# Modulations by column groups, an ordered first load and a buffer for the first projection weights, in a four-layer conditioned transformer

## The chip, the cores and the metric

The kernel runs on one core of one Trainium2 chip. The metric is the device time of one execution in microseconds (us), the median over runs. Engines are named as in the profile: PE is TensorE (PEld its weight loads), DVE VectorE, ACT ScalarE, POOL GpSimd, SP SyncE, which here issues every DMA.

## The reference

Sixteen sequences of 256 tokens with 256 features go through four transformer blocks, each conditioned on a vector per sequence. What concerns us is how the condition enters; layer 0, cut to that:

```
cond = silu(c) @ wc.T + bc                     # c: 16 x 256, wc: 1536 x 256
sh1, sc1, g1, sh2, sc2, g2 = split(cond, 6)
h = _ln(x) * (1 + sc1) + sh1;  x = x + g1 * attention(h)
h = _ln(x) * (1 + sc2) + sh2;  x = x + g2 * mlp(h)
```

Layers 1 and 2 are of the same kind, with a gain and an offset of the norm (`g1`, `be1`, ...) folded in, attention causal in layer 1 and with biases in layer 2. Layer 3 (called ROPE in the code) has no gates g; its condition goes through two products, `t1 = time_emb @ w_t1 + b_t1` (256 to 512 columns), then `(t1[:, :256] * silu(t1[:, 256:])) @ w_t2 + b_t2` (256 to 1024 columns), which give two scales and two shifts.

## The kernel before, in words

The program has two parts, each a block in which every engine has its own instruction list, with a barrier of all engines between them.

**The first part, here called the prologue,** makes everything that depends on the condition, for all four layers: COND, the scale and shift of each layer with features on the partitions (8 columns of 16 sequences per layer), and GR, the gate rows with sequences on the partitions, which go to DRAM (`gate_scratch`). SC is silu of the condition (L326 on ACT), stationary or moving with 16 columns. For each layer PE makes the gates (L353: the condition stationary, 256 weight columns moving, 4 products) and the scales and shifts (L360: 128 x 128 blocks of the weights stationary, the 16 columns of the condition moving, 16 products). L346 is the first product of ROPE. DVE turns the results into GR (L387, L391) and COND (L401 to L405, four short instructions for each of 4 feature halves, one waiting for another). In the lists the layers come as 0, 1, 2, ROPE. The loads are issued by SP on one queue in the order in which they are written: the weights CW of layer 0 (1536 KB), half of the input X (2048 KB), CW of layers 1 and 2, `cw_t1` and `cw_t2` of ROPE (they lie in the upper half of X until they are used), then the first projection weights through the two small buffers RAW, each buffer reused once its contents are split. An fp32 weight is split in two halves, "h" by ACT (`split_hi`, L252) and "l" by POOL or DVE (`split_lo`, L258), since the main part multiplies in fp32r. The upper half of X is loaded when the last layer's product is done (L306).

**The second part** is a software pipeline over 64 tiles (4 layers of 16 sequences). In step t the tile t+1 is normalised and projected to queries, keys and values (L948, L592, L924, L994, L483), tile t attends (L530 scores, L969 maxima, L729 transposed scores, L895 exponentials, L752 values), tile t-1 goes through the output projection and its norm, tile t-2 through the MLP. The first step is t = -2; in step -1 only tile 0 is projected. A table `plan` says in which step, and at which of three places in it (FIRST, EARLY, LATE), which chunk of the next weights is split; `load_raw` issues the loads for it. SP copies queries and keys into stacked operands QS and KS (L1356, 24 DMAs a tile) and the row maxima into QS (L1323). The order of work on each engine is fixed as written; nothing is scheduled at run time.

## Time and profile before

| | us |
|---|---|
| median of 3 runs (lowest, highest) | 2271.77 (2271.73, 2272.78) |
| the profiled execution, its own time | 2277.37 |
| its span in the profile | 2275.6 |
| PE busy in the span | 2175.1 (96%) |
| the prologue, from the span's start to the first instruction of the second part (DVE, 56.53) | 56.5 |
| the first main projection of PE (L483) starts at | 68.58 |

The page divides the span into busy time by engine and shows PE busy for 96% of it. It is an average: two stretches at the start are far from it, and the views by time show them. A wait is written in brackets behind the row, with the instruction or DMA that ended it.

### The profile page before, as it was taken

The numbers are of one execution on the slowest core, as the hardware profiler recorded it, in microseconds if no ns is written. First come the engines' busy times: TensorE is split into PE (matmuls) and PEld (weight loads), VectorE is DVE, ScalarE is ACT, GpSimd is POOL, SyncE is SP. The second block draws the span as 40 slices with busy tenths as digits, with TensorE's granted clock in tenths as the row PEclk, the third lists the DMA queues.
The fourth block names the chain that finished last, engine by engine and source line by source line (L and its number), as shares of the span: only waits on it lengthen the run. The fifth ranks groups of instructions, "written<-read, shape, count | busy, mean of one in ns | idle before, by whom it ended". The sixth has DMA issues, their size and how long they took to land.

```text
span 2275.6 us, 63435 instructions
## 1 busy us (share of the span) xinstructions
PE 2175.1 (96%) x20136; PEld 1830.7 (80%) x20136; DVE 1701.5 (75%) x4378; ACT 1251.0 (55%) x2620; POOL 1087.2 (48%) x1333
## 2 busy tenths in 40 slices
PE   7599999999999999999999999999999999999997
PEld 6478888888878888888878888888777878787877
DVE  3477777777777777777787777777888888888873
ACT  0356666666665556555676666666655443535341
POOL 1235544455445544454555544455454444444444
PEclk9899999999999999999999999999999999999999
DMA  6322222122322222112331222112222111211210
GB/s 200 110 69 65 67 70 72 64 63 81 95 81 64 68 70 67 62 62 92 90 99 64 70 74 67 63 61 80 82 79 65 59 64 60 61 64 58 68 57 15
DMA packets 164960, 166.12 MB, mean 73 GB/s; under 512 B 29328, under 2 KB 144400, under 8 KB 164848
## 3 DMA queue, kind: packets, MB, share of 16 engines
q1 hardware_dynamic: 164848, 164.69, 22.8%
q8 instruction: 63, 1.03, 0.2%
q14 instruction: 49, 0.40, 0.1%
HBM read 58.47 MB, written 4.39 MB: 28 GB/s over the span
## 4 chain that ended last, share of the span: by engine, by line
PE 84%; DVE 6%; issue 3%; SPq 2%; ACT 1%; DMA 1%; POOL 1%; POOLq 0%; ACTq 0%; DVEq 0%
PE B L483 36%; PE B L583 14%; PE B L752 10%; PE B L729 7%; PE B L530 7%; PE B L592 4%; PE B L602 2%; SPq L1356 2%; PE B L686 2%; DVE NEGM L969 2%; PE B L507 2%; DVE G L976 1%; ACT PR L895 1%; DMA RAW<-in_w 1%; ACT G L865 0%
## 5 line engine op out<-in xcount | busy, mean ns | idle before, releaser
L895 ACT ACTIVATE PR<-B 128x512 f32<-128x512 f32 (+1 forms) x1024 | 505.0, 570 | 285.0 <-PE B L729 282.2
L1251 POOL TENSOR_TENSOR GHl<-G,GHh 128x256 fp32r<-128x256 f32 x512 | 377.6, 738 | 476.2 <-ACT GHh L871 290.1
L969 DVE TENSOR_REDUCE NEGM<-B 128x2 f32<-128x512 f32 x768 | 485.1, 683 | 94.2 <-PE B L530 94.2
L483 PE MATMUL B<-H2h,W1h 128*128 128x256 f32 x1280 | 397.6, 311 | 3.1 <-issue 3.1
L483 PE MATMUL B<-H2h,W1l 128*128 128x256 f32 x1280 | 363.1, 284 | 0.0
L483 PE MATMUL B<-H2l,W1h 128*128 128x256 f32 x1280 | 362.5, 283 | 0.0
L871 ACT ACTIVATE G<-B,VEC 128x256 f32<-128x256 f32 x384 | 182.0, 474 | 284.4 <-PE B L483 284.4
L583 PE MATMUL B<-W2h,GHh 128*128 128x256 f32 x1024 | 296.8, 290 | 1.7 <-POOL GHl L1251 1.7
L583 PE MATMUL B<-W2l,GHh 128*128 128x256 f32 x1024 | 290.0, 283 | 0.0
L583 PE MATMUL B<-W2h,GHl 128*128 128x256 f32 x1024 | 289.4, 283 | 0.0
L483 PEld LDWEIGHTS B<-H2h,W1h 128*128 128x128 f32 x1280 | 244.4, 191 | 44.3 <-issue 26.2
L752 PE MATMUL B<-PR,V 128*32 128x256 f32 (+1 forms) x4096 | 262.2, 374 | 14.1 <-ACT PR L895 8.7
L483 PEld LDWEIGHTS B<-H2l,W1h 128*128 128x128 f32 x1280 | 245.3, 192 | 0.0
L483 PEld LDWEIGHTS B<-H2h,W1l 128*128 128x128 f32 x1280 | 244.4, 191 | 0.0
L1281 POOL TENSOR_TENSOR H2l<-HF,H2h 128x512 fp32r<-128x512 f32 x64 | 82.1, 1283 | 333.9 <-DVE H2h L1105 333.9
L729 PE MATMUL B<-QS,KS 64*128 64x256 f32 (+1 forms) x2048 | 211.6, 309 | 10.8 <-ACT PR L895 2.0
L530 PE MATMUL B<-KS,QS 48*128 48x256 f32 (+1 forms) x2048 | 199.0, 311 | 20.8 <-DMA KS<-KHL 13.2
L729 PEld LDWEIGHTS B<-QS,KS 64*128 64x128 f32 x2048 | 145.9, 186 | 82.5 <-ACT PR L895 48.3
L583 PEld LDWEIGHTS B<-W2h,GHh 128*128 128x128 f32 x1024 | 195.4, 191 | 10.3 <-DVE GHh L981 2.1
L966 DVE CUSTOM_DVE_ANT_0 B<-B,MASK 128x128 f32<-128x128 f32 (+1 forms) x512 | 165.8, 392 | 41.1 <-PE B L530 41.1
L583 PEld LDWEIGHTS B<-W2l,GHh 128*128 128x128 f32 x1024 | 196.0, 191 | 0.0
L583 PEld LDWEIGHTS B<-W2h,GHl 128*128 128x128 f32 x1024 | 195.9, 191 | 0.0
(149 smaller groups left out, 4753.1 us busy)
## 6 DMA issues: line engine op xcount, KB each, us to landing
QS<-QHL SPq DMA_DIRECT2D x768, 64.0 KB, 2.1
KS<-KHL SPq DMA_DIRECT2D x768, 64.0 KB, 2.1
GA<-gate_scratch SPq DMA_DIRECT2D x48, 256.0 KB, 3.2
GM<-gate_scratch SPq DMA_DIRECT2D x48, 256.0 KB, 3.5
RAW<-in_w SPq DMA_DIRECT2D x36, 256.0 KB, 3.1
CW<-in_cw SPq DMA_DIRECT2D x3, 1536.0 KB, 13.3
X<-in_x SPq DMA_DIRECT2D x2, 2048.0 KB, 10.4
QS<-MT SPq DMA_DIRECT2D x256, 4.0 KB
```

Of the source, the lines that this page charges most:

```text
L483: last = nc.tensor.matmul(dst, w[i], x[j], start=(first_k and n == 0), stop=(last_k and n == 2))
L530: last = nc.tensor.matmul(bank(banks[h])[:, i, 0:keys], QS[b:b + STK, p, i * P:(i + 1) * P], KS[b:b + STK, p, 0:keys], start=True, stop=True)
L583: last = nc.tensor.matmul(bank(7)[:, i, :], GH[x][:, j % RING, i * P:(i + 1) * P], W2[y][:, j, :], start=(j == 0 and n == 0 and i == 0), s ...
L592: last = nc.tensor.transpose(dst[:, f, i * P:(i + 1) * P], src[:, i, f * P:(f + 1) * P], IDENT[:])
L729: last = nc.tensor.matmul(B[:, banks[h], k * T:k * T + T - first], KS[b:b + ROWS, p, k * P:(k + 1) * P], QS[b:b + ROWS, p, first:T], start ...
L752: last = nc.tensor.matmul(bank(6 + g // 2)[32 * j:32 * j + 32, g % 2, c], V[:, k, HV * h:HV * h + 32], PR[:, h % PRING, k, 0:n], start=(k ...
L871: last = nc.scalar.activation(dst[:, j % RING, :], bank(3 - j % 2)[:, 0, :], ACT.Gelu, bias=VEC[:, s.lm, V_B1 + j:V_B1 + j + 1])
L895: nc.scalar.activation(PR[:, h % PRING].rearrange("p k q -> p (k q)")[:, 0:n], src[:, 0:n], ACT.Exp, scale=SCALE).then_inc(ac_exp, 1)
L966: last = nc.vector.tensor_tensor_reduce(src[:, i, 0:keys], src[:, i, 0:keys], unmasked, -1.0, HIGHEST, ALU.add, ALU.min, NEGM[:, i, c:c + 1])
L969: last = nc.vector.tensor_reduce(NEGM[:, :, c], src, op=ALU.max, axis=AX.X, negate=True)
L1251: nc.gpsimd.tensor_tensor(GH[1][:, j % RING, :], G[:, j % RING, :], GH[0][:, j % RING, :].bitcast(F32), ALU.subtract).then_inc(po_gl, 1)
L1281: nc.gpsimd.tensor_tensor(H2[1][:], HF[:], H2[0][:].bitcast(F32), ALU.subtract).then_inc(po_h2, 1)
```

## The change

It has three parts, and a shift of the plan that goes with them.

1. **Modulations.** The scales and shifts are made with the condition stationary, as the gates are: SC and Z3 are padded with zeros to 32 columns, and the four groups of 256 weight columns go to the four 32-column groups of PE's array (L366, 8 products of 32 x 256 per layer instead of 16 of 128 x 16). The result has sequences on the partitions; DVE copies it (MOD, L438), PE transposes it in two 128 x 128 pieces (L382), and DVE makes COND with 5 instructions of 64 elements (L445 to L451) instead of 16 of 16. The layers come as 0, 1, ROPE, 2, and in each the gates come behind the modulation on PE, and behind COND on DVE.
2. **Loads in another order.** One sequence of X only, then the first weights, then the layers as they are used, with `cw_t1` ahead of layer 1 and `cw_t2` ahead of layer 2; the rest of the lower half of X comes last. The upper half (2048 KB) and the gate rows' way to DRAM move into the second part.
3. **First projection weights** in buffers EQ and EO of their own, loaded whole and split with 3 instructions on ACT and POOL instead of 5 each through RAW.
4. In `plan` the four groups of MLP weights of layer 0 move by one step: from steps -1 and 0 to steps 0 and 1.

Core of the diff:

```diff

-        plan = {(-1, EARLY): part(0, "1", 0, 2), (-1, LATE): part(0, "2", 0, 1),
-                (0, EARLY): part(0, "1", 1, 3), (0, LATE): part(0, "2", 2, 3)}
+        plan = {(0, EARLY): part(0, "1", 0, 2), (0, LATE): part(0, "2", 0, 1),
...
+            EQ, EO = esb("EQ", [P, KD, WQ_COLS[0]]), esb("EO", [P, KD, D])
+            SC = esb("SC", [P, KD, 32])
...
+            Z3 = esb("Z3", [P, KD, 32])
+            MOD = [esb(f"MOD{i}", [P, D]) for i in range(2)]
...
+            t1tile = bank(7, 32)
+            LAYERS = (0, 1, ROPE, 2)
...
+                def modulation(l):
                     sp.dma_start(CW[l][:], a[f"cw{l}"].rearrange("(k p) n -> p k n", p=P)).then_inc(sp_cw[l], 16)
                     sp.dma_start(RB[l], a["rows"][l].partition_broadcast(NSEQ)).then_inc(sp_cw[l], 16)
...
+                sp.dma_start(CT[:], a["c_t"]).then_inc(sp_ct, 16)
+                sp.dma_start(VEC[:], a["vec"]).then_inc(sp_cw[0], 16)
+                sp.dma_start(IDENT[:], a["ident"]).then_inc(sp_cw[0], 16)
+                modulation(0)
+                sp.dma_start(X[:, 0:1], x_in[:, 0:1]).then_inc(sp_x[0], 16)
+                sp.dma_start(EQ[:], a["wq0"].rearrange("(k p) n -> p k n", p=P)).then_inc(sp_first[0], 16)
+                sp.dma_start(EO[:], a["wo0"].rearrange("(k p) n -> p k n", p=P)).then_inc(sp_first[1], 16)
                 sp.dma_start(CT1, a["cw_t1"].rearrange("(k p) n -> p k n", p=P)).then_inc(sp_cw[ROPE], 16)
+                modulation(1)
                 sp.dma_start(CT2, a["cw_t2"].rearrange("(k p) n -> p k n", p=P)).then_inc(sp_cw[ROPE], 16)
-                load_raw(sp, range(len(first_weights)))
-                sp.dma_start(IDENT[:], a["ident"]).then_inc(sp_const, 16)
+                modulation(2)
+                sp.dma_start(X[:, 1:8], x_in[:, 1:8]).then_inc(sp_x[1], 16)
                 sp.dma_start(ROT[:], a["rot"]).then_inc(sp_const, 16)
                 sp.dma_start(MASK[:], a["mask"]).then_inc(sp_const, 16)
...
-                sp.dma_start(X[:, 8:16], x_in[:, 8:16]).then_inc(sp_x[1], 16)
-                sp.wait_ge(sp_gs, 16)
-                sp.wait_ge(sp_x[0], 16)
-                sp.wait_ge(sp_const, 64)
-
...
+                nc.gpsimd.memset(SC[:], 0.0).then_inc(po_init, 1)
+                nc.gpsimd.memset(Z3[:], 0.0).then_inc(po_init, 1)
...
+                for k in range(KD):
+                    po.wait_ge(ac_first, k + 1)
+                    nc.gpsimd.tensor_tensor(WQ[0][1][:, k, :], EQ[:, k, :], WQ[0][0][:, k, :].bitcast(F32),
+                                            ALU.subtract).then_inc(po_first, 1)
...
+                nc.scalar.activation(SC[:, :, 0:NSEQ], CT[:], ACT.Silu).then_inc(ac_silu, 1)
+                ac.wait_ge(sp_first[0], 16)
+                for k in range(KD):
+                    nc.scalar.activation(WQ[0][0][:, k, :], EQ[:, k, :], ACT.Copy).then_inc(ac_first, 1)
+                ac.wait_ge(sp_first[1], 16)
+                nc.scalar.activation(WO[0][:], EO[:], ACT.Copy).then_inc(ac_first, 1)
...
+                def conditioning():
+
+                    pe.wait_ge(sp_cw[ROPE], 32)
+                    for f in range(2 * KD):
+                        for k in range(KD):
+                            last = nc.tensor.matmul(t1tile[:, f, :], CT1[:, k, f * P:(f + 1) * P], CT[:, k, :],
+                                                    start=(k == 0), stop=(k == KD - 1))
+                    last.then_inc(pe_t1, 1)
+
+                def modulation(l):
+
+                    w, m = (CT2, Z3) if l == ROPE else (CW[l], SC)
+                    for k in range(KD):
+                        for c, c0 in enumerate(starts[l]):
+                            last = nc.tensor.matmul(B[32 * c:32 * c + 32, l, 0:D], m[:, k, :], w[:, k, c0:c0 + D],
+                                                    start=(k == 0), stop=(k == KD - 1))
+                    last.then_inc(pe_mod, 1)
+
...
+                    for r, c0 in enumerate((2 * D, 5 * D)):
+                        for k in range(KD):
+                            last = nc.tensor.matmul(bank(4 + l)[0:NSEQ, r, :], SC[:, k, 0:NSEQ], CW[l][:, k, c0:c0 + D],
+                                                    start=(k == 0), stop=(k == KD - 1))
+                    last.then_inc(pe_gates, 1)
...
+                    pe.wait_ge(dv_mod, n + 1)
+                    for f in range(KD):
+                        last = nc.tensor.transpose(bank(l, 4)[:, 2 + f, :], MOD[n % 2][:, f * P:(f + 1) * P], IDENT[:])
+                    last.then_inc(pe_cond, 1)
+
+                pe.wait_ge(ac_silu, 1)
+                pe.wait_ge(po_init, 2)
+                for n, l in enumerate(LAYERS):
                     if l == ROPE:
-                        for f in range(2 * KD):
-                            for k in range(KD):
...
-                        pe.wait_ge(vz, KD)
+                        pe.wait_ge(dv_t1, KD)
                     else:
...
-                    w, m = (CT2, Z3) if l == ROPE else (CW[l], SC)
-                    for c, c0 in enumerate(starts[l]):
-                        for f in range(KD):
-                            for k in range(KD):
-                                last = nc.tensor.matmul(ctile[l][:, 2 * c + f, :],
-                                                        w[:, k, c0 + f * P:c0 + (f + 1) * P], m[:, k, :],
-                                                        start=(k == 0), stop=(k == KD - 1))
-                    last.then_inc(pm, 1)
+                        pe.wait_ge(sp_cw[l], 64 if l == 0 else 32)
...
+                    modulation(l)
+                    if l != ROPE:
+                        gates(l)
+                    to_features(n, l)
+                    if n == 0:
+                        conditioning()
...
+                        dv.wait_ge(ac_t1, KD)
...
-                            nc.vector.scalar_tensor_tensor(Z3[:, k, :], t1tile[:, k, :], VEC[:, ROPE, V_T1 + k:V_T1 + k + 1],
-                                                           SLU[:, k, :], ALU.add, ALU.mult).then_inc(vz, 1)
-                    else:
...
-
-                    dv.wait_ge(pm, 1 + l)
...
-                            chain(nc.vector.tensor_scalar(U[:, f, :], ctile[l][:, tile, :], vec(sc), 1.0, ALU.add, ALU.add))
-                            chain(nc.vector.tensor_scalar(U2[:, f, :], ctile[l][:, tile + KD, :], vec(sh), None, ALU.add))
-                            settle()
-                            chain(nc.vector.tensor_scalar(COND[:, l, cs + f, :], U[:, f, :], vec(g), None, ALU.mult))
-                            chain(nc.vector.scalar_tensor_tensor(COND[:, l, cb + f, :], U[:, f, :], vec(be), U2[:, f, :],
-                                                                 ALU.mult, ALU.add))
-                            settle()
...
+                            nc.vector.scalar_tensor_tensor(Z3[:, k, 0:NSEQ], t1tile[:, k, :], VEC[:, ROPE, V_T1 + k:V_T1 + k + 1],
...
+                    dv.wait_ge(pe_mod, i + 1)
+                    nc.vector.tensor_copy(MOD[i % 2][:], B[:, l, 0:D]).then_inc(dv_mod, 1)
+                    dv.wait_ge(pe_cond, i + 1)
...
+                    chain(nc.vector.tensor_tensor(U[:], sc, SCP[:, l].unsqueeze(3).to_broadcast([P, 2, KD, NSEQ]), ALU.add))
+                    chain(nc.vector.tensor_tensor(U2[:], sh, shift, ALU.add))
+                    settle()
+                    chain(nc.vector.tensor_tensor(cond[:, :, 0], U[:], gain, ALU.mult))
+                    chain(nc.vector.tensor_tensor(U3[:], U[:], offset, ALU.mult))
+                    settle()
+                    chain(nc.vector.tensor_tensor(cond[:, :, 1], U3[:], U2[:], ALU.add))
+                    settle()
+                    if l != ROPE:
+                        gate_rows(l, l + 1)
...
+                    if isinstance(a_, int) and a_ == 0:
+                        ac.wait_ge(sp_gs, 16)
...
+                    if isinstance(tile, int) and tile in (0, 1, 3):
+                        dv.wait_ge(sp_x[(0, 1, None, 2)[tile]], 16)
...
+                    if isinstance(s.q, int) and s.q == 0:
+                        sp.dma_start(X[:, 8:16], a["x"].rearrange("s (t p) d -> p s t d", p=P)[:, 8:16]).then_inc(sp_x[2], 16)
+                        sp.wait_ge(sp_const, 48)
...
+            sp.wait_ge(dv_rows, 6)
+            sp.dma_start(g_scr.rearrange("l s r d -> s l r d"), GR).then_inc(sp_gs, 16)
```

The first place is PE in the prologue. Of before, all layers but the last product (CW and `X<-in_cw_t` are the weights, SC the condition, `sp_cw3` the semaphore that both ROPE weights raise):

```order
L353 MATMUL B<-CW,SC 16x256 x3
L360 MATMUL B<-SC,CW 128x16 x16
L353 MATMUL B<-CW,SC 16x256 [waits sp_cw1]
L353 MATMUL B<-CW,SC 16x256 x3
L360 MATMUL B<-SC,CW 128x16 x16
L353 MATMUL B<-CW,SC 16x256 [waits sp_cw2]
L353 MATMUL B<-CW,SC 16x256 x3
L360 MATMUL B<-SC,CW 128x16 x16
L346 MATMUL B<-CT,X 128x16 [waits sp_cw3]
L346 MATMUL B<-CT,X 128x16 x7
L360 MATMUL B<-Z,X 128x16 [waits dv_t1]
```

Now, from the transposes of layer 0 to those of ROPE:

```order
L382 MATMUL B<-IDENT,MOD 128x128 [waits dv_mod]
L382 MATMUL B<-IDENT,MOD 128x128
L357 MATMUL B<-CT,X 128x16 [waits sp_cw3]
L357 MATMUL B<-CT,X 128x16 x7
L366 MATMUL B<-CW,SC 32x256 [waits sp_cw1]
L366 MATMUL B<-CW,SC 32x256 x7
L374 MATMUL B<-CW,SC 16x256 x4
L382 MATMUL B<-IDENT,MOD 128x128 [waits dv_mod]
L382 MATMUL B<-IDENT,MOD 128x128
L366 MATMUL B<-X,Z 32x256 [waits dv_t1]
L366 MATMUL B<-X,Z 32x256 x7
L382 MATMUL B<-IDENT,MOD 128x128 [waits dv_mod]
```

The block product (L360) is gone, and two waits stand in PE's list that did not: the ROPE product L357 waits for both ROPE weights ahead of layer 1, and each pair of transposes waits for DVE's copy.

The second place is DVE from the barrier to the first tile's query. Before (XQ is the normalised tile, W1l the low half of an MLP weight):

```order
L935 BN_STATS ST<-X 128x6 x2
L940 BN_AGGR MV<-ST 128x2 [waits dv_st1]
L940 BN_AGGR MV<-ST 128x2
L258 TENSOR_TENSOR W1l<-RAW,W1h 128x512 [waits ac_w] x2
L948 TENSOR_SCALAR XQ<-X,MV,RS 128x256 [waits po_rs1]
L948 TENSOR_SCALAR XQ<-X,MV,RS 128x256
L994 CAST H1h<-HF 128x512 [waits ac_h1]
L1198 CAST QHL<-B 128x512 [waits pe_q]
```

Now:

```order
L984 BN_STATS ST<-X 128x6 [waits sp_x0]
L984 BN_STATS ST<-X 128x6
L989 BN_AGGR MV<-ST 128x2 [waits dv_st1]
L989 BN_AGGR MV<-ST 128x2
L997 TENSOR_SCALAR XQ<-X,MV,RS 128x256 [waits po_rs1]
L997 TENSOR_SCALAR XQ<-X,MV,RS 128x256
L1043 CAST H1h<-HF 128x512 [waits ac_h1]
L1247 CAST QHL<-B 128x512 [waits pe_q]
```

The two splits W1l ahead of XQ are gone from here; the next pair comes in step 0 as before, and there is one more pair in step 1.

The third place is SP from the first tile's last key copies to the row maxima (MT) of tile 0. Before, and behind it now:

```order
L1356 DMA KS<-KHL 16x4x256 [waits dv_k]
L1356 DMA KS<-KHL 16x4x256 x5
L239 DMA RAW<-in_w 128x2x256 [waits dv_w] x2
L1323 DMA QS<-MT 1x4x256 [waits ac_mt]
L1323 DMA QS<-MT 1x4x256
L1331 DMA GA<-gate_scratch 128x512
L1323 DMA QS<-MT 1x4x256 [waits ac_mt]
```

```order
L1407 DMA KS<-KHL 16x4x256 [waits dv_k]
L1407 DMA KS<-KHL 16x4x256 x5
L1411 DMA X<-in_x 128x16x256
L240 DMA RAW<-in_w 128x2x256 [waits dv_w,sp_const]
L240 DMA RAW<-in_w 128x2x256 [waits dv_w]
L1372 DMA QS<-MT 1x4x256 [waits ac_mt]
L1372 DMA QS<-MT 1x4x256
L1382 DMA GA<-gate_scratch 128x512 [waits sp_gs]
```

The 2048 KB of X stand between the key copies and the loads of W2 (`RAW<-in_w 128x2x256`), and ahead of the rows of maxima.

## Rows read from the trace of the kernel before

**Rows 1.** Windows of the prologue's middle: busy us (instructions) of each engine, PEclk, DMA

```profile
20.00:30.00 10.00, 10.00 (x39) 7.47 (x40) 4.49 (x20) 1.03 (x2) 1.00 (x2) 1.00 0.81 298
```

**Rows 2.** Timeline of the prologue: start, us, engine, what [idle before <-releaser]

```profile
9.83 3.57 PE L353 MATMUL B<-CW,SC 128*16 128x256 f32 x8 [9.83 <-ACT SC L326]
13.33 7.01 PE L360 MATMUL B<-SC,CW 128*128 128x16 f32 x32
13.44 0.74 DVE L387 TENSOR_TENSOR PR<-B,PR 16x256 f32<-16x256 f32 x2 [13.44 <-PE B L353]
14.22 0.74 DVE L391 TENSOR_TENSOR PR<-PR 16x256 f32<-16x256 f32 x2
...
41.12 3.57 PE L346 MATMUL B<-CT,X 128*128 128x16 f32 x16
...
45.27 0.38 DVE L381 SCALAR_TENSOR_TENSOR Z<-B,VEC,SLU 128x16 f32<-128x16 f32 x2 [0.71 <-ACT SLU L332]
...
55.76 0.23 DVE L405 SCALAR_TENSOR_TENSOR COND<-U,VEC 128x16 f32<-128x16 f32 x1
```

**Rows 3.** Timeline, SP's issues of three loads in the prologue

```profile
2.13 0.46 SPq L292 DMA_DIRECT2D PR<-in_rows  x1
...
3.11 6.05 SPq L291 DMA_DIRECT2D CW<-in_cw  x1
...
11.53 0.47 SPq L296 DMA_DIRECT2D X<-in_cw_t  x1
```

**Rows 4.** DMA issues: KB, us from issue to landing, of the first and third of these

```profile
PR<-in_rows SPq DMA_DIRECT2D x1, 64.0 KB, 7.3
```

```profile
X<-in_cw_t SPq DMA_DIRECT2D x1, 1024.0 KB, 16.4
```

**Rows 5.** Timeline at 414 us, the column groups of L752 and the weight load behind

```profile
414.39 1.07 PE L752 MATMUL B<-PR,V 128*32 128x256 f32 x16
```

```profile
415.39 0.54 PEld L729 LDWEIGHTS B<-QS,KS 64*128 64x128 f32 x8 [0.41 <-ACT PR L895]
```

**Rows 6.** Windows of PE's projections: PE's busy us (x), then the others, PEclk, DMA

```profile
71.00:72.00 1.00, 1.00 (x7) 1.00 (x6) 0.48 (x1) 0.00 (x0) 0.00 (x0) 1.00 0.71 223
95.00:96.00 1.00, 1.00 (x7) 1.00 (x7) 1.00 (x2) 0.73 (x2) 0.71 (x1) 0.50 0.01 4
98.00:99.00 1.00, 1.00 (x10) 1.00 (x9) 0.70 (x2) 1.00 (x3) 0.00 (x0) 1.00 0.00 0
```

**Rows 7.** Timeline of the first tile

```profile
58.12 0.71 POOL L1222 TENSOR_TENSOR RS<-TV,HALF 128x2 f32<-128x2 f32 x1
...
62.40 1.35 DVE L258 TENSOR_TENSOR W1l<-RAW,W1h 128x512 fp32r<-128x512 f32 x2 [4.77 <-ACT W1h L252]
63.66 0.73 DVE L948 TENSOR_SCALAR XQ<-X,MV,RS 128x256 f32<-128x256 f32 x2
64.45 1.12 PE L592 MATMUL B<-IDENT,XQ 128*128 128x128 f32 x4 [11.75 <-DVE XQ L948]
```

**Rows 8.** DMA issues at 52.7 and at 56.5 us: KB, us to landing

```profile
X<-in_x SPq DMA_DIRECT2D x1, 2048.0 KB, 8.3
```

```profile
RAW<-in_w SPq DMA_DIRECT2D x2, 256.0 KB, 5.3
```

**Rows 9.** Timeline around these issues and in step 0

```profile
52.73 0.40 SPq L306 DMA_DIRECT2D X<-in_x  x1
...
56.50 14.77 SPq L239 DMA_DIRECT2D RAW<-in_w  x6
...
89.54 1.10 SPq L239 DMA_DIRECT2D RAW<-in_w  x2
...
94.60 1.13 ACT L252 ACTIVATE W2h<-RAW 128x512 fp32r<-128x512 f32 x2
...
97.74 0.60 ACT L895 ACTIVATE PR<-B 128x512 f32<-128x512 f32 x1 [2.02 <-PE B L729]
```

**Rows 10.** Timeline of DVE in step 1

```profile
113.99 1.88 DVE L969 TENSOR_REDUCE NEGM<-B 128x2 f32<-128x512 f32 x3
115.78 0.73 DVE L948 TENSOR_SCALAR XQ<-X,MV,RS 128x256 f32<-128x256 f32 x2
117.16 0.69 DVE L1152 TENSOR_TENSOR TOK<-B,GA 128x512 f32<-128x512 f32 x1 [0.64 <-PE B L483]
```

More of the change, by code:

```diff
@@ L141, in bank @@
             return B[:, n, :].rearrange("p (a b) -> p a b", a=parts)
-        sp_x = [sem(f"sp_x{half}") for half in range(2)]
+        sp_x = [sem(f"sp_x{part}") for part in range(3)]
+        sp_ct, sp_first = sem("sp_ct"), [sem(f"sp_first{x}") for x in "qo"]
+        ac_first, po_first = sem("ac_first"), sem("po_first")
         sp_const, sp_cw, sp_gs = sem("sp_const"), [sem(f"sp_cw{l}") for l in range(NL)], sem("sp_gs")
@@ L323, in _ @@
+                po.wait_ge(ac_first, KD + 1)
+                nc.gpsimd.tensor_tensor(WO[1][:], EO[:], WO[0][:].bitcast(F32), ALU.subtract).then_inc(po_first, 1)
+                po.wait_ge(po_first, KD + 1)
+                po.wait_ge(po_init, 7)
             @block.scalar
             def _(ac):
[L325 to L328 removed]
@@ L494, in weights @@
             def weights(l, what, first_tile, *which):
-                if not (isinstance(first_tile, int) and first_tile == 0):
+                if not (isinstance(first_tile, int) and first_tile == 0) or (l == 0 and what in "qo"):
                     return
```

100 lines of the change are left out of this document (41 added, 59 removed).

## The prediction

> **What bounds the kernel now.** I read the busy time first: PE is busy for 96% of the span, so what can be won lies where PE works on something that could be shorter, or where it stands still. The view by time shows two such places, both ahead of the steady part. The first is the prologue. In its middle PE is busy for 10.00 of 10.00 us while the DMA engines are only 0.81 busy [rows 1], so PE bounds it. Per layer it spends 3.57 us on the gates and 7.01 us on the modulation [rows 2]; with 3.57 us for the first product of ROPE, that is 3 x 3.6 + 4 x 7.0 + 3.6 = 42.4 of the 46 us from PE's first product at 9.83 to the last COND instruction at 55.99. The second place is the first tile: its normalisation factor is ready at 58.83 (58.12 + 0.71), but DVE first stands at W1l, for which ACT waited on a load, and normalises only at 63.66 [rows 7].
>
> **PE's pace.** The projection products run at 7 per us at 71 us and at 95 us, and at 10 per us at 98 us [rows 6]. At 95 us the granted clock is 0.50 (1.2 GHz), at 98 us 1.00 (2.4 GHz). At 71 us the column says 1.00, yet the pace is that of 0.50. So ahead of about 80 us I go by pace, not by the column, and take the prologue to run at the low level: an fp32 product of 256 columns is two records of 0.446 us there (3.57 / 8) [rows 2].
>
> **The modulation product.** Before shows no group of this form in the prologue. The nearest row is L752, the same shape (128 rows, 32 columns, 256 moving, fp32, four column groups, 16 records), which takes 1.00 us from its start to the next weight load, the 0.41 us of changing the form included [rows 5]. That row is at the high level, so at the low one I take 2.0 us. Bounds: 1.0 us if the level were high, 16 x 0.446 = 7.1 us if the groups ran one after another. I take 2.0, since L752 shows them side by side. The two transposes are half of the four of L592, 1.12 us: 0.6 us [rows 7]. The DVE copy of 256 columns is half of XQ's 0.73, 0.4 us.
>
> **When can PE start?** Between the landing of the rows of layer 0 (2.13 + 7.3 = 9.4 us) and that of `cw_t2` (11.53 + 16.4 = 27.9 us) came 6784 KB, 367 KB per us [rows 3, 4]. Now 64 KB of IDENT stand ahead: layer 0 starts at 9.6. But PE's list then has the first ROPE product, and its wait is for both ROPE weights. Behind layer 0 come 256 + 768 + 256 + 512 + 1536 + 64 + 1024 = 4416 KB until `cw_t2` is in, 12.0 us: 21.6. PE is through with layer 0 at 9.6 + 2.0 + 3.6 + 0.6 = 15.8 and stands still for 5.8 us. So the loads set the first half of the new prologue, and layer 0 costs nothing.
>
> **The path from there,** each term from rows 2, 5 and 7: ROPE's first product 3.6 (25.2); layer 1's modulation 2.0 (27.2), gates 3.6, in which DVE's copy is hidden (30.8), transposes 0.6 (31.4). Then DVE: COND in 5 instructions. Those of 16 elements take 0.23, those of 256 elements 0.37 us [rows 2]; for 64 I take 0.28, 1.4 in all (bounds 1.2 and 1.9), to 32.8. Gate rows 0.74 + 0.74 (34.3). Only now Z, 0.4 (34.7), because it stands behind layer 1 in DVE's list, and PE waits for it. ROPE's modulation 2.0 (36.7), the copy 0.5 with its hand-over, here hidden by nothing (37.2), transposes 0.6 (37.8). Layer 2: 2.0, 3.6, 0.6 (44.0), COND 1.4, gate rows 1.5 (46.9). The barrier took 0.5 from DVE's last instruction to the second part; that makes 47.4 against 56.5. **Minus 9.1.** If the loads were later, the whole path would move with them.
>
> **The first tile.** XQ no longer stands behind W1l: from 58.83 instead of 63.66, **minus 4.8** [rows 7]. What comes next on that path (transposes, scale and shift, projection) is as before and waits for nothing that the change makes late: X's first sequence and the weights landed long ago, and the splits of the first weights on ACT and POOL have from about 12 us to 47 us.
>
> **What is given back in step 0.** SP issues the upper half of X behind the last key copy, in before's time at 89.5, where it issued the loads of W2 [rows 9]. Alone in the queue such a transfer took 8.3 us, and the loads issued behind it at 56.5 landed 5.3 us later, at 61.8, that is 0.8 us behind its end at 61.0 [rows 8, 9]. So X lands at 97.8 and W2 at 98.6 to 99.3. ACT has both W2h splits (1.13) ahead of its exponentials, and the rows of maxima, for which PE's transposed scores wait, are issued behind on the same queue. The first exponential goes from 97.74 to about 100.3: **plus 2.5**. Bounds: 0 if the small loads passed X, and 6 more if SP itself is held, as it was for 6.05 us at the issue behind the first half of X [rows 3]; I take neither, since the queue is nearly empty here.
>
> **Step 1** gets what step -1 lost: two W1l splits of 1.35 us in all [rows 7] ahead of XQ on DVE. DVE was idle for 0.64 us there before TOK [rows 10], so **plus 0.7**; behind TOK the maxima wait, and PE's scores for them. The other two pairs (W2h on ACT, W2l on POOL) fall, as I take it, into idle time; were they not covered, the ACT pair would cost 1.1 [rows 9]. The gate rows' store, now first in SP's second list, and the wait for it are over before step 0: nothing.
>
> **Sum:** -9.1 - 4.8 + 2.5 + 0.7 = -10.7. The profiled execution's own time is 2277.37, so 2266.7 for one like it. It lies 5.6 above the median of 2271.77; by the median the forecast is **2261.1 us**, 0.47% less. Chance 0.62, with 2258 to 2265 as its own range. About 0.2% (4.5 us) is what a measurement of this kernel can tell from no change.
>
> **Rivals.**
> *The loads stay late.* The product that opens the path waits for `cw_t2`; if SP is held again for 6.05 us [rows 3] while the queue runs dry, `cw_t2` lands as before at 27.9: 6.3 later, 2267.4. Against it: the queue held work throughout before, in spite of that hold. Chance 0.09.
> *Step 0 loses more.* PE stands for 2.5 us at a place where its clock has just gone from 0.50 to 1.00. If it falls back, the 10 us of work left in step 0 run in part at half pace: 5 more, 2266. For it: the clock was down at 95 us after a stretch of waits [rows 6]. Against: the stall is short. Chance 0.11.
> *PE gets its high level in the prologue.* Then from layer 1's gates on everything on PE halves: (3.6 + 0.6 + 2.0 + 0.6 + 2.0 + 3.6 + 0.6) / 2 = 6.5 less, 2254.6. Against it: PE was busy without a break and its pace was flat at 0.446 per record [rows 1, 2], and now it has more gaps; for it: four column groups use more of the array at a time. Chance 0.12. The Trainium skill, TensorE: Matmul & The Clock Gate, Part 1: The HAM clock gate, says that a TensorE kept busy is given its full clock, which speaks for this rival; this trace, 43 us of unbroken work at the low pace, does not agree.
> *The groups run one after another, and it gets slower.* One mechanism: a modulation costs 7.1 instead of 2.0 in layers 1, ROPE and 2 (in layer 0 the wait for `cw_t2` hides it), 15.3 more: -10.7 + 15.3 = +4.6, 2276.4. It decides from 2.0 + 10.7 / 3 = 5.6 us per modulation on: from there nothing is won. Against it stands L752 [rows 5]; for it only that both the clock level and the operands differ. Chance 0.06.
>
> **The range** takes in the first three rivals and leaves out the last: 2254 to 2267.5. Faster by over 0.2%: the forecast, the high level, the loss in step 0 and half of the late loads, with a little off for the sum of small errors, 0.86; within 0.2%: 0.08; slower: 0.06.
>
> **What the changed profile would show.** The second part's first DVE instruction at about 47.4; PE idle from about 15.8 to 21.6, ended by the load of `cw_t2`; the 16 records of L366 in 2.0 us; a wait of PE for Z at about 31.4 to 34.7; XQ 2.4 us behind the second part's start instead of 7.1; X's upper half landing some 8 us after its issue, with ACT's W2h waiting for it and the first exponential late by 2.5; two W1l in step 1 with TOK late by 0.7; and from step 2 on the same tile times as before. I would be wrong if the modulation takes over 5 us, if `cw_t2` lands past 26, or if the steady part itself changes, for which I see no reason: no instruction of it is touched.

## The result, and the profile after

The changed kernel takes 2260.66 us (median of 5 runs, 2259.35 to 2262.32), the kernel before 2271.77 (5 runs, 2270.32 to 2272.85): ratio 0.9949, 95% interval 0.9936 to 0.9962, so 0.51% faster. The profiled execution of the changed kernel has its own time of 2262.32 (span 2260.4), 15.05 less than that of the kernel before. That is more than the 11.1 between the medians; the first experiment shows why.

First the prologue: timeline of the changed kernel, columns as in [rows 2].

```profile
10.21 1.94 PE L366 MATMUL B<-CW,SC 128*32 128x256 f32 x16 [10.21 <-DMA PR<-in_rows]
11.88 2.63 PE L374 MATMUL B<-CW,SC 128*16 128x256 f32 x8
...
15.31 1.81 DVE L448 TENSOR_TENSOR COND<-U,VEC 128x64 f32<-128x64 f32 x1
21.55 3.60 PE L357 MATMUL B<-CT,X 128*128 128x16 f32 x16 [6.67 <-DMA X<-in_cw_t]
25.08 1.94 PE L366 MATMUL B<-CW,SC 128*32 128x256 f32 x16
26.79 3.62 PE L374 MATMUL B<-CW,SC 128*16 128x256 f32 x8
...
30.84 0.22 DVE L445 TENSOR_TENSOR U<-B,SCP 128x64 f32<-128x64 f32 x1 [3.33 <-PE B L382]
31.62 0.23 DVE L451 TENSOR_TENSOR COND<-U 128x64 f32<-128x64 f32 x1
...
33.34 0.36 DVE L435 SCALAR_TENSOR_TENSOR Z<-B,VEC,SLU 128x16 f32<-128x16 f32 x2
33.75 1.90 PE L366 MATMUL B<-X,Z 128*32 128x256 f32 x16 [2.95 <-DVE Z L435]
36.18 0.69 PE L382 MATMUL B<-IDENT,MOD 128*128 128x128 f32 x2 [0.53 <-DVE MOD L438]
36.80 1.93 PE L366 MATMUL B<-CW,SC 128*32 128x256 f32 x16
38.51 2.96 PE L374 MATMUL B<-CW,SC 128*16 128x256 f32 x8
...
43.70 0.75 DVE L422 TENSOR_TENSOR PR<-PR,G 16x256 f32<-16x256 f32 x2
44.78 0.75 DVE L984 BATCH_NORM_STATS2 ST<-X 128x6 f32<-128x256 f32 x2 [0.33 <-PEq L262]
47.12 0.74 DVE L997 TENSOR_SCALAR XQ<-X,MV,RS 128x256 f32<-128x256 f32 x2 [1.23 <-POOL RS L1271]
52.03 0.55 PE L530 MATMUL B<-H1h,WQ0h 128*128 128x256 f32 x1 [3.01 <-POOL H1l L1341]
```

A modulation is 16 records in 1.94 us, with the next product 1.7 behind its start, where there were 32 records in 7.01 [rows 2]. PE has two long waits: 6.67 us until `cw_t2` has landed, and 2.95 us for Z, which DVE makes only behind COND and the gate rows of layer 1. The second part starts at 44.78 instead of 56.53. XQ follows 2.34 us later, behind POOL's RS alone; the W1l that stood ahead of it [rows 7] is gone. The first projection comes 7.25 us behind the start of the second part, against 12.05 before.

The DMA issue of `cw_t2` in the changed kernel (KB, us from issue to landing; it was issued at 6.91, so it lands at 21.5):

```profile
X<-in_cw_t SPq DMA_DIRECT2D x1, 1024.0 KB, 14.6
```

Step 0 and step 1 in the timeline of the changed kernel, the places of [rows 9] and [rows 10]:

```profile
71.86 0.59 SPq L1411 DMA_DIRECT2D X<-in_x  x1
72.54 2.45 SPq L240 DMA_DIRECT2D RAW<-in_w  x2
73.35 1.22 PE L577 MATMUL B<-KS,QS 48*128 48x256 f32 x8 [1.31 <-DMA KS<-KHL]
...
81.37 1.36 ACT L253 ACTIVATE W2h<-RAW 128x512 fp32r<-128x512 f32 x2 [4.35 <-DMA RAW<-in_w]
81.74 1.22 PE L776 MATMUL B<-QS,KS 64*128 64x256 f32 x8 [1.97 <-DMA QS<-MT]
82.64 0.60 ACT L944 ACTIVATE PR<-B 128x512 f32<-128x512 f32 x1
96.74 0.42 DVE L1053 TENSOR_TENSOR TOK<-B,RZ 128x256 f32<-128x256 f32 x1
101.34 1.29 DVE L259 TENSOR_TENSOR W1l<-RAW,W1h 128x512 fp32r<-128x512 f32 x2
...
103.19 0.69 DVE L1201 TENSOR_TENSOR TOK<-B,GA 128x512 f32<-128x512 f32 x1
```

Its DMA issues between 71 and 78 us, to be read against [rows 8]:

```profile
X<-in_x SPq DMA_DIRECT2D x1, 2048.0 KB, 8.7
RAW<-in_w SPq DMA_DIRECT2D x2, 256.0 KB, 8.3
```

X's upper half sits at the head of the queue. Behind it wait W2, for which ACT stands 4.35 us, and the row maxima MT (4 KB each), for which PE's transposed scores stand 1.97 us. The first exponential comes 9.29 us behind the first score product (82.64 - 73.35). Before, it came 6.72 behind: 97.74 in [rows 9], less the start of this score product:

```profile
91.02 1.23 PE L530 MATMUL B<-KS,QS 48*128 48x256 f32 x8 [2.42 <-DMA KS<-KHL]
```

So the lead over the profiled execution before is 11.75 us at the start of the second part, 16.55 at the first projection (68.58 - 52.03), 17.67 at the first score product of tile 0 (91.02 - 73.35; in the profile before, one of the issues of the key copies took 1.71 us, here none did), 15.10 at the first exponential, 13.97 at step 1's TOK (117.16, [rows 10]). From there to the end of the span it is 2158.4 before and 2157.2 after.

### The profile page after: what moved, and what is told of

Read it like the earlier page. It is cut to its first block, busy times and chain, and to the rows that moved or that the text cites. A ratio compares the mean times of both kernels' runs of the same rounds, so it can differ in the third digit from the quotient of the medians.

```text
span 2260.4 us, 63283 instructions
## 1 busy us (share of the span) xinstructions
PE 2155.1 (95%) x20080; PEld 1807.2 (80%) x20080; DVE 1697.4 (75%) x4339; ACT 1249.8 (55%) x2618; POOL 1086.4 (48%) x1333
## 4 chain that ended last, share of the span: by engine, by line
PE 84%; DVE 6%; issue 3%; SPq 2%; ACT 1%; POOL 1%; DMA 1%; POOLq 0%; ACTq 0%; DVEq 0%
PE B L530 36%; PE B L630 14%; PE B L799 10%; PE B L776 7%; PE B L577 7%; PE B L639 4%; PE B L649 2%; PE B L733 2%; DVE NEGM L1018 2%; SPq L1407 2%; PE B L554 2%; DVE G L1025 1%; ACT PR L944 1%; ACT G L912 0%; POOL GHl L1300 0%
## 5 line engine op out<-in xcount | busy, mean ns | idle before, releaser
L799 PE MATMUL B<-PR,V 128*32 128x256 f32 (+1 forms) x4096 | 262.9, 375 | 14.1 <-ACT PR L944 8.7
```

The lines of the kernel that those rows point to most:

```text
L799: last = nc.tensor.matmul(bank(6 + g // 2)[32 * j:32 * j + 32, g % 2, c], V[:, k, HV * h:HV * h + 32], PR[:, h % PRING, k, 0:n], start=(k ...
```

## The experiments

**The kernel before, again.** No edit.

> The kernel before, unchanged, profiled once more. The profiled execution of before that the prediction's sum was made against took 2277.37 us, 5.6 above the median of its runs. Theory A (that execution was long by chance, in the stretches ahead of step 2): the new profile's own time is within 2 us of 2271.8, and its first exponential comes earlier than 97.74 us. Theory B (a profiled execution of this program is always some 5 us longer): about 2277 again.

Measured: 2271.82 us, ratio 1.0005 (0.9993 to 1.0018). Its profiled execution took 2270.68, 6.7 less than the first one, and its first exponential comes at 91.56, as theory A has it. It looks different in the prologue (timeline of PE):

```profile
13.34 4.10 PE L360 MATMUL B<-SC,CW 128*128 128x16 f32 x32
19.99 3.56 PE L353 MATMUL B<-CW,SC 128*16 128x256 f32 x8 [2.55 <-DMA OR<-in_rows]
23.48 4.01 PE L360 MATMUL B<-SC,CW 128*128 128x16 f32 x32
...
30.62 4.29 PE L360 MATMUL B<-SC,CW 128*128 128x16 f32 x32
34.74 3.57 PE L346 MATMUL B<-CT,X 128*128 128x16 f32 x16
39.33 7.01 PE L360 MATMUL B<-Z,X 128*128 128x16 f32 x32 [1.01 <-DVE Z L381]
```

Three of the four L360 groups, 7.01 us each in the first profile, take 4.0 to 4.3 here. PE's windows of this execution (PE busy us, records, granted clock, DMA share, GB/s) show why: the clock is up for most of such a group and falls to 0.50 within it, although PE is busy throughout.

```profile
23.00:26.80 3.80, 3.80 (x32) 0.95 1.03 379
26.80:30.00 3.20, 3.20 (x11) 0.50 0.38 134
30.00:33.60 3.60, 3.60 (x30) 0.97 0.40 109
33.60:38.00 4.40, 4.40 (x23) 0.50 0.43 128
```

The second part starts at 50.17 instead of 56.53: 6.4 of the 6.7 us. The first profiled execution was a long one, because PE had the low level in the whole prologue.

In step 0 the first exponential of this execution comes 7.19 us behind the first score product (which starts at 84.37), not 6.72:

```profile
91.56 0.60 ACT L895 ACTIVATE PR<-B 128x512 f32<-128x512 f32 x1 [2.48 <-PE B L729]
```

**The shift of the plan alone.** On the kernel before:

```diff
-        plan = {(-1, EARLY): part(0, "1", 0, 2), (-1, LATE): part(0, "2", 0, 1),
-                (0, EARLY): part(0, "1", 1, 3), (0, LATE): part(0, "2", 2, 3)}
+        plan = {(0, EARLY): part(0, "1", 0, 2), (0, LATE): part(0, "2", 0, 1),
+                (1, EARLY): part(0, "1", 1, 3), (1, LATE): part(0, "2", 2, 3)}
```

> The kernel before with part 4 of the change alone: the first MLP weights are split one step later. Theory (W1l ahead of XQ held the first tile): XQ 2.4 us behind the start of the second part instead of 7.1, minus 4.8, and plus 0.5 to 0.7 in step 1, so minus 4.1 to 4.3 and about 2267.6 us; no collision in step 0, since the upper half of X is still loaded at the end of the prologue. Rival (the first tile waits for the next thing, the transfer of X or the copies of queries and keys, so the gain is lost): 2271 to 2272.

Measured: 2267.23 us, ratio 0.9985 (0.9971 to 0.9999), 3.7 below the median of its set (2270.95). XQ stands 2.33 us behind the start of the second part (55.27 and 52.94), as in the changed kernel, and the first projection 7.24 us behind that start instead of 12.00 in the second profile of before. So the first tile's gain is shown by itself in the trace. In the time the net of it and of what step 1 gives back is 3.7 us in the median, and the interval allows from nothing to 6.6.

**The changed kernel with the old modulations.** Loads, order of the layers, buffers and plan of the changed kernel, but the blocks of weights stationary again (the core of the edit; COND is made from the result as before, without MOD and its transposes):

```diff
-                    for k in range(KD):
-                        for c, c0 in enumerate(starts[l]):
-                            last = nc.tensor.matmul(B[32 * c:32 * c + 32, l, 0:D], m[:, k, :], w[:, k, c0:c0 + D],
+                    for c, c0 in enumerate(starts[l]):
+                        for f in range(KD):
+                            for k in range(KD):
+                                last = nc.tensor.matmul(bank(l, 32)[:, 2 * c + f, :],
+                                                        w[:, k, c0 + f * P:c0 + (f + 1) * P], m[:, k, 0:NSEQ],
```

> The changed kernel with the modulations as in the kernel before: 16 products with 128 x 128 weight blocks stationary, no copy, no transposes, COND in 16 short instructions. Loads, buffers, layer order and plan as changed. Theory (the column groups are what the prologue gains by, the loads alone bring nothing since PE had no wait before): behind the landing of the second ROPE weight at 21.5 us come 3.5 + 10.6 + 7.0 + 10.6 of PE work with a wait for Z in between, the prologue ends at about 57 instead of 44.8, and the time is about 2273 us. Rival (the loads bring most, because PE starts the work in time and layer 0 is hidden): 2262 to 2266.

Measured: 2273.85 us, ratio 1.0005 (0.9994 to 1.0016). Without the new modulations the whole change brings nothing: the old products take 6.98, 6.99, 5.71 and 6.99 us, the wait for `cw_t2` shrinks to 1.01 us since PE is busy until then, and the second part starts at 54.82. The loads are not priced alone here. The run has the first tile's gain in it, and the place of X in step 0 as well (its first exponential comes 9.76 us behind the first score product); it lies 6.6 us above the run with the shift of the plan alone (2267.23). By the ratios of the changed kernel (0.9949 to 0.9958, which is 2259 to 2261 on this set's 2270.95), the new modulations are worth 12 to 15 us with these loads.

**The condition stationary, but no column groups.** The zeros around the condition are widened to 128 columns, so that each of the 8 products of a layer fills all output rows and the four pieces add up in one result; the same columns move, one product behind the other (SC and Z3 get four shifted copies of the condition for it):

```diff
-                            last = nc.tensor.matmul(B[32 * c:32 * c + 32, l, 0:D], m[:, k, :], w[:, k, c0:c0 + D],
-                                                    start=(k == 0), stop=(k == KD - 1))
+                            last = nc.tensor.matmul(B[:, l, 0:D], m[:, k, P * c:P * c + P], w[:, k, c0:c0 + D],
+                                                    start=(k == 0 and c == 0), stop=(k == KD - 1 and c == 3))
```

> The changed kernel with the modulations' four column groups made into four full products: the condition stands in 128 stationary columns, zero except for the group's 16, and all 8 products of a layer accumulate into one 128 x 256 result. Same result, same copy, transposes and COND; only the overlap of the groups is gone. Theory (groups run side by side, PE at the low level): a modulation takes 16 x 0.445 = 7.1 us instead of 1.8, 5.3 more in each of layers 1, ROPE and 2, layer 0 hidden: plus 16, about 2276.5 us. Rival (with the whole array in use PE's clock goes to its high level early): a modulation takes about 3.6 us and gates halve too, plus 2 to 5, 2263 to 2266.

Measured: 2271.26 us, ratio 1.0000 (0.9989 to 1.0011), between the two expectations. The modulations take 6.37, 6.13, 5.41 and 3.62 us, not 7.1 each, as the clock rises during them; all gates take 1.90, wholly at the high level. Side by side the same 16 records take 1.94 at the low level; at the high level they take 1.07 (in the profile of the next run), where these take 3.62. This is what the rival on the other side of the forecast would have looked like: with the groups in series, the gain is gone.

**The changed kernel, again.** No edit.

> The changed kernel once more, on the same chip as the three variants of it below, so that they are compared with many runs of it. Theory (TensorE's clock level in the prologue differs from one execution to the next, as the two profiles of the kernel before show, whose second parts start at 56.53 and 50.17 us): about 2260.7 us in the median, and the second part starts within 2 us of 44.8. Rival (the first profile of it was a lucky one): a second part's start 3 us or more later.

Measured: 2263.12 us against 2271.45, ratio 0.9958 (0.9942 to 0.9974). The second part starts at 42.65, and the first exponential comes 9.64 us behind the first score product. The start is 0.1 us outside the expected 2 us around 44.8. PE's clock is up in other places than in the first profile of this kernel: ROPE's modulation takes 1.07 instead of 1.90 us.

**The upper half of X in the prologue.** The issue is moved from step 0 to SP's first list, behind ROPE's modulation, which is the last to read the weights that lie there.

```diff
+                sp.wait_ge(pe_mod, 3)
+                sp.dma_start(X[:, 8:16], x_in[:, 8:16]).then_inc(sp_x[2], 16)
...
-                        sp.dma_start(X[:, 8:16], a["x"].rearrange("s (t p) d -> p s t d", p=P)[:, 8:16]).then_inc(sp_x[2], 16)
```

> The changed kernel with the upper half of X issued at the prologue's end, as soon as ROPE's modulation is done, instead of behind the first tile's key copies. Theory (in step 0 the 2048 KB stand ahead of the W2 loads and the rows of maxima, and cost 2.5): the first exponential comes 6.7 us behind the first product of the second half of the scores, as in the kernel before, instead of 9.3; minus 2.5 against the changed kernel. Rival (something else then ends that wait): no difference.

Measured: 2257.74 us, ratio 0.9934 (0.9918 to 0.9949); five of its six runs lie below the fastest of the changed kernel on that chip (2260.93). X is issued at 35.29. In step 0 (timeline) neither ACT's W2h nor PE's L778 waits for a DMA any more:

```profile
72.90 1.22 PE L579 MATMUL B<-KS,QS 48*128 48x256 f32 x8 [1.32 <-DMA KS<-KHL]
76.47 1.14 ACT L253 ACTIVATE W2h<-RAW 128x512 fp32r<-128x512 f32 x2
79.26 1.22 PE L778 MATMUL B<-QS,KS 64*128 64x256 f32 x8
80.16 0.60 ACT L946 ACTIVATE PR<-B 128x512 f32<-128x512 f32 x1 [2.54 <-PE B L778]
```

The first exponential is 7.26 us behind the first score product, against 9.29 to 9.85 in three profiles of the changed kernel, and 7.19 in the second profile of before. The transfer's place costs 2.0 to 2.6 us there. From the first score product to step 1's TOK it is 27.92 us here and 29.84, 31.48 and 31.35 in those three, so 1.9 to 3.6 us in all: part of the price comes behind the first exponential, where PE's clock rises later in the changed kernel (see step 0 in the next section). The medians differ by 5.4; where the rest comes from is not settled.

**ROPE's first product waits for its own weights only.**

```diff
-                sp.dma_start(CT1, a["cw_t1"].rearrange("(k p) n -> p k n", p=P)).then_inc(sp_cw[ROPE], 16)
+                sp.dma_start(CT1, a["cw_t1"].rearrange("(k p) n -> p k n", p=P)).then_inc(sp_ct1, 16)
...
-                    pe.wait_ge(sp_cw[ROPE], 32)
+                    pe.wait_ge(sp_ct1, 16)
...
                         pe.wait_ge(dv_t1, KD)
+                        pe.wait_ge(sp_cw[ROPE], 16)
```

> The changed kernel with ROPE's first product waiting for its own weight alone, not for the second ROPE weight as well. Theory (this wait, 6.7 us on PE, is what holds the path): PE runs the product at about 15 instead of 21.5, layer 1 starts at about 18.5 instead of 25.1, the prologue ends 6.5 earlier, minus 6.5. Rival (the weights of layers 1 and 2 then end the waits, or DVE does): minus 2 to 4.

Measured: 2256.76 us, ratio 0.9926 (0.9910 to 0.9942), 6.4 below the changed kernel; all six runs are below its fastest. L357 starts at 14.36, and PE now waits 2.65 us for the rows of layer 1, until 18.96. Layer 1 starts 6.4 us earlier, the second part at 37.72, 4.9 us before that of the changed kernel beside it (42.65); between the two PE has less of the high level here (layer 1's gates take 3.58 us against 2.46, ROPE's modulation 1.94 against 1.07). The wait for `cw_t2` was on the path that sets the end.

**Z ahead of layer 1 on DVE.**

```diff
-                    if l == ROPE:
+                    if l == 1:

                         dv.wait_ge(ac_t1, KD)
```

> The changed kernel with the Z instructions of DVE ahead of layer 1's COND and gate rows instead of behind them. Theory: PE's wait of 2.9 us for Z between layer 1 and ROPE is gone, but the copy of ROPE's modulation then waits for the gate rows of layer 1, minus 2.3. Rival (DVE is the bound of this stretch anyway): less than 1.

Measured: 2256.78 us, ratio 0.9929 (0.9913 to 0.9944), 6.3 below the changed kernel where the wait itself is 2.95. Timeline of PE behind layer 1's gates:

```profile
26.88 2.34 PE L374 MATMUL B<-CW,SC 128*16 128x256 f32 x8
...
29.52 1.07 PE L366 MATMUL B<-X,Z 128*32 128x256 f32 x16
32.58 0.44 PE L382 MATMUL B<-IDENT,MOD 128*128 128x128 f32 x2 [2.00 <-DVE MOD L438]
32.95 1.07 PE L366 MATMUL B<-CW,SC 128*32 128x256 f32 x16
33.84 1.89 PE L374 MATMUL B<-CW,SC 128*16 128x256 f32 x8
```

The wait is gone, a wait of 2.00 us for MOD has come in place of one of 0.55 (DVE still does COND and the gate rows of layer 1 first), and what follows runs at the high level: L366 in 1.07 us and the gates in 1.89, against 1.78 and 2.93 in the profile of the changed kernel beside it. So in the trace the order of DVE's list is worth 2.95 - 1.45 = 1.5 us, and the clock 1.7; the second part starts at 39.04, 3.6 us earlier. The median moved by more than that, and the trace does not show where the rest comes from.

**The changed kernel, a third time,** beside the next two.

> The changed kernel as it is, for comparison on the same chip with the next two. Expected near its earlier medians of 2260.7 and 2263.1 us: 2260 to 2264. First DVE instruction of the second part between 42.5 and 45 us, the first exponential of tile 0 some 9.3 to 9.6 us behind its first score product, with the upper half of X issued between them.

Measured: 2262.27 us against 2273.11, ratio 0.9952 (0.9934 to 0.9969); second part from 43.53, the first exponential 9.85 us behind its first score product, a little more than expected.

**The rest of the lower half of X ahead of the first weights.**

```diff
+                sp.dma_start(X[:, 1:8], x_in[:, 1:8]).then_inc(sp_x[1], 16)
                 sp.dma_start(EQ[:], a["wq0"].rearrange("(k p) n -> p k n", p=P)).then_inc(sp_first[0], 16)
...
-                sp.dma_start(X[:, 1:8], x_in[:, 1:8]).then_inc(sp_x[1], 16)
                 sp.dma_start(ROT[:], a["rot"]).then_inc(sp_const, 16)
```

> The changed kernel with the other seven sequences of the lower half of X (1792 KB) loaded ahead of the first weights, so ahead of cw_t1, layer 1 and cw_t2, instead of behind layer 2. Theory (the loads set the first half of the new prologue, at 367 KB per us): cw_t2 lands 4.9 us later, at about 26.4, PE waits about 11.5 us for it instead of 6.7, and everything behind moves by 4.9: 4.9 us above the changed kernel's median of the same set, second part from about 49. Rival (the load order is worth nothing, as it was worth nothing with the old products, because PE makes the wait good by a higher clock level behind it): within 1.5 us of the changed kernel. Second rival (SP is held at an issue, as it was for 6.05 us behind the first half of X in the kernel before): over 6 us.

Measured: 2268.79 us, ratio 0.9978 (0.9966 to 0.9990), 6.5 above the changed kernel of the same set. Its timeline:

```profile
4.34 5.63 SPq L304 DMA_DIRECT2D EQ<-in_wq  x1
27.20 3.59 PE L357 MATMUL B<-CT,X 128*128 128x16 f32 x16 [11.77 <-DMA X<-in_cw_t]
49.36 0.75 DVE L984 BATCH_NORM_STATS2 ST<-X 128x6 f32<-128x256 f32 x2 [0.33 <-PEq L262]
```

The product starts 5.4 us later than in the changed kernel of the same set (21.78), and the second part 5.8 later. SP is held for 5.63 us at an issue behind the large load, as in [rows 3], and it costs little: the DMA engines are 0.97 busy meanwhile, and 4.9 of the 5.4 us are the 1792 KB. The median moved by 6.5, which is also what the second rival asked for (over 6); the trace speaks against it, since it leaves the hold 0.5 us at most. With the new modulations a load ahead of `cw_t2` costs what its bytes take.

**Filling PE's wait.** Six more products of the gates' form, whose result nobody uses, between layer 0 and the wait for `cw_t2`:

```diff
+                    for i in range(6):
+                        nc.tensor.matmul(bank(7)[0:NSEQ, i % 2, :], SC[:, i % KD, 0:NSEQ], CW[0][:, i % KD, 0:D], start=True, stop=True)
                     pe.wait_ge(sp_cw[ROPE], 32)
```

> The changed kernel with six more products of the gates' form (condition stationary, 256 weight columns of layer 0 moving, result overwritten and used by nobody) on PE behind layer 0, where PE stood still for 6.1 to 6.7 us waiting for cw_t2; 12 records of 0.446 us are 5.4 us at the low level, so they end before cw_t2 lands. Nothing else is touched. Theory (a TensorE that has been working until cw_t2 lands more often gets its high level behind it): the products of ROPE and layer 1 behind the wait take half the time in the profiled execution or in a good part of the others, and the median falls by 2 to 6 us against the changed kernel's 0.9949 to 0.9958 of the kernel before, so a ratio of 0.993 to 0.9945. Rival (the level does not hang on this idle time; the kernel before had PE busy without a break and stayed low in its first profile): the ratio stays at 0.995 to 0.996, L357 takes 3.6 us.

Measured: 2262.79 us against 2269.42, ratio 0.9968 (0.9958 to 0.9978): no gain over the 0.9949 to 0.9958 of the changed kernel. Timeline of PE:

```profile
15.68 2.76 PE L355 MATMUL B<-CW,SC 128*16 128x256 f32 x12
21.42 2.81 PE L359 MATMUL B<-CT,X 128*128 128x16 f32 x16 [2.98 <-DMA X<-in_cw_t]
24.16 1.94 PE L368 MATMUL B<-CW,SC 128*32 128x256 f32 x16
```

The extra products ran at the high level, so they filled only 2.8 us, and 3 us of idle time were left. L359, which began at the high level (the granted clock was 1.00 until past 22 us), took 2.81 instead of 3.60 us, and the modulation behind it 1.94 again. Work put in so as to raise the clock brought nothing in the median. As the wait was only half filled, the run does not say what a wait wholly filled would do.

**All three edits together.** Upper half of X in the prologue, ROPE's first product waiting for its own weights, Z ahead of layer 1.

> The changed kernel with the three single edits together: upper half of X issued behind ROPE's modulation in the prologue, the first ROPE product waiting for cw_t1 alone, and Z made ahead of layer 1 in DVE's list. Theory (each takes away a wait of its own, and these lie one behind another): 6.5 for the wait on cw_t2, 2.3 to 2.95 for the wait on Z, 2.5 for the transfer in step 0, so 11.3 us or more below the changed kernel of the same set, about 2250, second part from about 35. By the sum of what the three gave alone (6.4 + 6.3 + 5.4, the last two above their waits since more of PE's work ran at the high level) it would be 18 below, 2244. Rival (two of the three take away the same time, for example because layer 1's weights, which landed at about 18.9, hold everything behind): 8 below or less, 2254.

Measured: 2251.39 us (2245.78 to 2253.88), ratio 0.9900 (0.9883 to 0.9917) to the kernel before, and 10.9 below the changed kernel of its set; all six runs are below the fastest of either kernel. Timeline of the prologue:

```profile
14.80 1.86 PE L359 MATMUL B<-CT,X 128*128 128x16 f32 x16
18.82 1.94 PE L368 MATMUL B<-CW,SC 128*32 128x256 f32 x16 [2.16 <-DMA OR<-in_rows]
...
27.63 0.58 PE L384 MATMUL B<-IDENT,MOD 128*128 128x128 f32 x2 [2.00 <-DVE MOD L441]
35.72 0.75 DVE L987 BATCH_NORM_STATS2 ST<-X 128x6 f32<-128x256 f32 x2 [0.33 <-PEq L262]
```

The second part starts 7.8 us earlier than in the changed kernel beside it (43.53), and the first exponential is 7.25 instead of 9.85 us behind the first score product: 7.8 + 2.6 = 10.4. The 7.8 can be followed in the two traces. Layer 1 starts 6.5 us earlier (18.82 against 25.31), 2.16 us of waiting for its rows included. Its gates take 0.9 more (3.62 against 2.68). The wait of 2.94 for Z is gone, the one for MOD has grown by 1.45 (2.00 against 0.55), and ROPE's modulation takes 0.9 less, at the high level. The 18 us of the three gains added do not come. This is the fastest kernel of the study.

## Why the prediction was right, step by step

**The prologue, forecast -9.1.** The landing of `cw_t2` (21.6 forecast, 21.5 read), PE's idle time until then, the modulation (2.0; 1.94), the transposes, Z as the last of DVE's work for layer 1 and PE's wait for it are there as forecast, and two experiments show both waits on the path. The second part began at 44.78, not 47.4. Of these 2.6 us, 0.6 are the modulations of layers 1 and 2 (1.7 from start to start instead of 2.0), 0.8 COND in the same two layers (1.0 instead of 1.4), 0.6 the clock (layer 2's gates took 2.96 instead of 3.6) and 0.2 the barrier (0.33 instead of 0.5); the rest is spread over the transposes and hand-overs. One reading behind these terms was wrong and did no harm: the 0.41 us in [rows 5] are no change of form, the row says that the weight load waited for PR of ACT. The 2.0 us of a modulation held (1.94).

**The step that did not hold** is "I ... take the prologue to run at the low level". It was read off one execution in which it was true. In another execution of the same program it was not, and in the changed kernel the gates of layers 0 and 2 ran in part at the high level. So the rival that PE gets its high level in the prologue was neither absent nor whole, and it touches both kernels. (The 43 us of work without a break, which the prediction set against it, had a break: PE waited 1.01 us for Z ahead of 45.70.) Against the long execution that the prediction was read from, the second part starts 11.75 us earlier; against the second profile of before, where it starts at 50.17, it starts 5.4, 7.5 and 6.6 us earlier (44.78, 42.65 and 43.53), not 9.1. Subtracting a sum made in a long execution from the median of the kernel before had no ground.

**That the number came out so well is in part luck.** The three sets of runs (ratios 0.9949, 0.9958 and 0.9952, that is 8.3 to 11.1 us less) lie close to the forecast 10.7. The traces do not bear out its sum: set against the second profile of before, the three profiles of the changed kernel lead by 7.2 to 7.9 us at step 1's TOK and by 5.3 to 8.5 at the end of the span; set against the first one, the first of them leads by 13.97 and 15.2. The forecast lies between two kinds of execution, and so do the medians of the kernel before, which mix them (last section).

**The first tile, forecast -4.8:** 12.05 - 7.25 = 4.80.

**Step 0, forecast +2.5:** 9.29 - 6.72 = +2.57 between the first profiles, and 2.1 to 2.7 between the 7.19 of the second profile of before and the 9.29, 9.64 and 9.85 of the changed kernel. The mechanism is the one named, the transfer of X ahead of W2 and of the row maxima in the same queue, and it is gone when X is loaded elsewhere. In the changed kernel of the third set ACT waits 0.69 us for PE at this place and no longer for W2, so the maxima bind there.

The rival *Step 0 loses more*, priced at 5 us, came true in part. In both profiles of before the granted clock is back at 1.00 by 0.1 us behind the first exponential; in the three of the changed kernel it comes back 2.4, 5.4 and 4.7 us behind it. From the first exponential to the last TOK of step 0 it is 13.4 and 13.5 us before (97.74 to 111.18, 91.56 to 105.10), and 14.1, 15.4 and 15.1 after: 0.6 to 2.0 more.

**Step 1, forecast +0.7:** the lead goes from 14.44 (at the TOK of 96.74, which in the trace of before is at 111.18) to 13.97, +0.5. In the second profile of before DVE's idle time ahead of this TOK is 0.17 us, not the 0.64 of [rows 10], and against that one it is +1.0.

**Not forecast:** the 1.1 us between the first projection and the first score product. That stretch takes 22.15 to 22.47 us in all four profiles with the old modulations and 21.3 in the ten others; why is not shown. The late loads and the groups in series did not occur; without groups the gain was zero, not a loss of 4.6, because the clock rose during the longer products.

## What to carry to other kernels

A profile is one execution of the program: before its durations are set against a median, see how its own time lies to it, and take a second one where a stretch hangs on the clock. A small load behind a large one in the same queue lands with the large one (256 KB of W2 8.3 us after the issue, where it took 3.0 without X ahead of it), so a transfer that nobody awaits belongs where nothing urgent is issued behind it. When products get several times shorter, the order of the lists and of the loads sets the end: PE stood 6.7 us at a wait for two loads where one would do, and 3 us while DVE did work that nobody awaited ahead of what PE awaits.

## What was unexpected of the hardware

**The clock level of a stretch differs between executions of one program.** In one execution of the kernel before, PE worked for 43 us at the pace of 1.2 GHz; in another it rose to 2.4 GHz three times and fell back each time (at 16.6, 26.8 and 33.6 us), always while PE worked on. The Trainium skill, TensorE: Matmul & The Clock Gate, Part 1: The HAM clock gate, says that a TensorE kept busy is given its full clock, and that how many products run before it varies from run to run. The second profile agrees as to the rise, not as to the falls in the midst of work; the first shows no rise in 43 us of work. What decides it stays open.

How often the long kind of execution comes can be estimated from the mean granted clock that is on record for every run. The record reads 1.00 until its first change, whatever PE's pace; that change came at 79.9 us in the first profile (mean 0.989) and at 16.6 us in the second (0.978). Of the 79 runs of the kernel before in four sets, 22 have a mean of 0.987 or more, and they took 2274.0 to 2279.0 us; the other 57 have 0.982 or less and a median of 2269.5. That the 22 had the low level in the whole prologue is inferred from the two profiles, not shown, and it need not be the only cause of the spread.

**DVE's short instructions in layer 0's COND** took 1.81 us at L448, where the same instruction takes 0.23 us in layer 1, and L449 behind it took 1.30 instead of 0.22. POOL was splitting the first weights at the time (3.57 us from 13.47, 1.26 from 17.00), and both DVE instructions end within 0.1 us of one of POOL's. L445 and L446, which read one operand from B in PSUM, took 0.22 and 0.21 us beside the same work of POOL. It is off the path here; that POOL is the cause was not tried.
